# Fused linear attention and mixture-of-experts layer on one core: identity matmuls ahead of the tokens, a reordered start, and a shorter Newton step

## The reference, cut to what matters

```python
xn = _layernorm(x)                                   # (2, 512, 512) tokens
# attention: 32 heads of 128, causal, a decay per head
qkv = silu(xn @ qkv_w.T)
attn = linear_attention_with_decay(q, k, v)          # exp(-slope * distance) on the scores
attn = attn * rsqrt(mean(attn * attn, -1) + 1e-5)    # over all 4096 columns
a = (sigmoid(xn @ gate_w.T) * (norm_w * attn)) @ out_w.T
# experts: router, best 2 of 8, low-rank experts
logits = xn @ W_router.T
h = xn @ A ; hw = h * combine
f = xn @ W_base.T + b_base + 2 * hw @ B
return x + a + f
```

## Time and profile before

| | |
|---|---|
| median of 3 runs | 1084.96 us (1084.82 to 1085.02) |
| the profiled execution | 1084.91 us, its span 1083.0 us |
| busy share of the span: PE, PEld | 99%, 87% |
| DVE, ACT, POOL | 66%, 63%, 59% |
| chain that ended last, by engine | PE 95%, ACT 1%, DVE 1%, DMA 1%, POOL 1%, issue 1% |

### The profile page before, as it was taken

The page is one execution under the profiler, slowest core; times in us unless marked ns, Lnnn a source line. Parts: engine busy times, 40 slices in busy tenths (PEclk is TensorE's granted clock), DMA queues, the critical chain, the costliest instruction groups (busy, mean ns, idle before and its releaser), DMA issues.

```text
span 1083.0 us, 18994 instructions
## 1 busy us (share of the span) xinstructions
PE 1069.0 (99%) x5902; PEld 941.9 (87%) x5902; DVE 715.0 (66%) x1209; ACT 686.2 (63%) x1401; POOL 635.3 (59%) x625
## 2 busy tenths in 40 slices
PE   6999999999999999999999999999999999999998
PEld 5898889888898888988898888988889888898897
DVE  7777674666657676675756667475755757557567
ACT  8677565765667565675756766576656756567532
POOL 4747563584637657375544846367473764647744
DMA  8212020120201201021101102012020211112222
GB/s 300 66 35 93 25 64 20 45 64 25 64 19 54 71 25 62 3 84 39 56 32 44 63 24 63 19 44 63 24 71 12 82 44 44 44 38 71 60 82 78
DMA packets 41605, 60.04 MB, mean 55 GB/s; under 512 B 3936, under 2 KB 21600, under 8 KB 41568
## 3 DMA queue, kind: packets, MB, share of 16 engines
q1 hardware_dynamic: 40992, 59.01, 17.1%
q10 hardware_dynamic: 576, 0.56, 0.2%
HBM read 52.74 MB, written 6.82 MB: 55 GB/s over the span
## 4 chain that ended last, share of the span: by engine, by line
PE 95%; ACT 1%; DVE 1%; DMA 1%; POOL 1%; issue 1%; SPq 0%; DVEq 0%; POOLq 0%
PE bank_q L1809 8%; PE bank_q L1811 8%; PE bank_q L1810 8%; PE bank_p L1809 6%; PE bank_p L1811 6%; PE bank_p L1810 5%; PE bank_r L1809 5%; PE bank_r L1811 5%; PE bank_r L1810 5%; PE outp L1809 5%; PE outp L1810 5%; PE outp L1811 5%; PE score L1811 3%; PE score L1810 3%; PE score L1809 3%; PE att L1811 3%
## 5 line engine op out<-in xcount | busy, mean ns | idle before, releaser
L415 POOL TENSOR_TENSOR w_lo<-combo,w_hi 128x768 fp32r<-128x768 f32 (+1 forms) x128 | 166.7, 1311 | 155.4 <-ACT w_hi L611 155.3
L415 POOL TENSOR_TENSOR w_lo<-raw,w_hi 128x256 fp32r<-128x256 f32 (+1 forms) x128 | 131.9, 1032 | 123.9 <-ACT w_hi L611 123.4
L466 POOL TENSOR_TENSOR sum_sq<-sum_sq,square 128x512 f32<-128x512 f32 x64 | 82.7, 1293 | 65.4 <-ACT square L760 65.4
L1372 DVE TENSOR_TENSOR acc<-acc,outp 128x512 f32<-128x512 f32 x116 | 79.4, 684 | 62.1 <-PE outp L1811 61.3
L1810 PE MATMUL bank_q<-c_lo,w_hi 128*128 128x512 f32 x276 | 107.4, 389 | 0.0
L1811 PE MATMUL bank_q<-c_hi,w_lo 128*128 128x512 f32 x276 | 107.4, 389 | 0.0
L1809 PE MATMUL bank_q<-c_hi,w_hi 128*128 128x512 f32 x276 | 107.4, 389 | 0.0
L1282 DVE TENSOR_TENSOR score<-score,table 128x512 f32<-128x512 f32 (+1 forms) x128 | 75.9, 627 | 40.6 <-PE score L1811 39.6
L1230 DVE TENSOR_TENSOR xs<-bank_r,xs 128x512 f32<-128x512 f32 x64 | 44.2, 691 | 88.6 <-ACT xs L611 60.9
L611 ACT ACTIVATE p_hi<-score 128x896 fp32r<-128x896 f32 (+1 forms) x128 | 81.1, 649 | 33.7 <-DVE score L1282 33.0
L1809 PE MATMUL outp<-wo_hi,g_hi 128*128 128x512 f32 x250 | 97.7, 391 | 0.2 <-DVE acc L1372 0.2
(11 more groups left out here) (295 smaller groups left out, 3470.2 us busy)
## 6 DMA issues: line engine op xcount, KB each, us to landing
raw<-w_chunks SPq DMA_DIRECT2D x165, 256.0 KB, 2.8
near_dram<-near SPq DMA_DIRECT2D x2, 2048.0 KB, 8.9
table<-near_dram SPq DMA_DIRECT2D x32, 128.0 KB, 2.0
y<-x SPq DMA_DIRECT2D x8, 256.0 KB, 3.8
out<-acc SPq DMA_DIRECT2D x7, 256.0 KB, 2.0
acc<-x SPq DMA_DIRECT2D x6, 256.0 KB, 7.4
acc<-x ACTq DMA_DIRECT2D x2, 256.0 KB, 3.9
hw_dram<-acc SPq DMA_DIRECT2D x1, 512.0 KB, 2.9
```

Of the source, the lines that this page charges most:

```text
L415: pool.tensor_tensor(piece(w_lo[i % 2], j), piece_source(i, j), piece(w_hi[i % 2], j).bitcast(F32), ALU.subtract).then_inc(wlo[j], 1)
L466: pool.tensor_tensor(sum_sq[:, s % 2, :], sum_sq[:, s % 2, :], square[:], ALU.add).then_inc(summed, 1)
L1372: dve.tensor_tensor(tile, tile, outp, ALU.add).then_inc(acc_done, 1)
```

## The change

TensorE multiplies the identity by itself 16 times before it waits for the first tokens. Tiles 0 and 1 are loaded in halves by two queues. `slope` and `norm` move from ScalarE's queue to the end of SyncE's first loads. `refine` has 3 operations in place of 4. q and k of batch 0 are made by passes over both (high parts of everything first). ScalarE makes one decay table fewer ahead of the first weights, and copies all 8 token tiles before `first_q(0)`; V1's weights come after. GpSimd's `combine(V1)` waits until all tiles are normalised, and the token sum `t_raw[:, 2]` goes ahead of V1's low parts. VectorE does `first_lows(0)` after the first token sum. `first_gates(1, 1)` goes ahead of V2's weights. In the last body `make_c22(G01)` goes ahead of `inverse_root(1, 1)`.

```diff
 @block.sync
-            for t in (0, 2):
-                sp.dma_start(acc[:, t, :], x_tok[:, t, :]).then_inc(x_in[t], 16)
+            for t in range(2):
+                sp.dma_start(acc[0:P // 2, t, :], x_tok[0:P // 2, t, :]).then_inc(x_in[t], 16)
+            sp.dma_start(acc[:, 2, :], x_tok[:, 2, :]).then_inc(x_in[2], 16)
             load_rows(0, 0, 3)
...
             sp.dma_start(ar[:], a_router).then_inc(ar_in, 16)
+            sp.dma_start(slope[:], slopes.rearrange("(a h) -> a h", a=1).to_broadcast([P, HEADS])).then_inc(slope_in, 16)
+            sp.dma_start(norm[:], norm_w).then_inc(norm_in, 16)
 @block.gpsimd
+            pool.wait_ge(xn_ready, NTB)
             combine(V1)
+            pool.wait_ge(xt_done, NTB)
+            pool.tensor_tensor(t_raw[:, 2], x_t[:, 2:4, 1, :], x_t[:, 0:2, 1, :], ALU.subtract).then_inc(t3_made, 1)
             low(V1, 2)
             low(V1, 4)
-            pool.wait_ge(xt_done, NTB)
-            pool.tensor_tensor(t_raw[:, 2], x_t[:, 2:4, 1, :], x_t[:, 0:2, 1, :], ALU.subtract).then_inc(t3_made, 1)
 @block.scalar
-            for t in (1, 3):
-                act.dma_start(acc[:, t, :], x_tok[:, t, :]).then_inc(x_in[t], 16)
-            act.dma_start(slope[:], slopes.rearrange("(a h) -> a h", a=1).to_broadcast([P, HEADS])).then_inc(slope_in, 16)
-            act.dma_start(norm[:], norm_w).then_inc(norm_in, 16)
+            for t in range(2):
+                act.dma_start(acc[P // 2:P, t, :], x_tok[P // 2:P, t, :]).then_inc(x_in[t], 16)
+            act.dma_start(acc[:, 3, :], x_tok[:, 3, :]).then_inc(x_in[3], 16)
-            nears(range(16))
+            nears(range(15))
             act.wait_ge(raw_in[0], 32)
...
             tokens_hi(0)
+            nears((15,))
+            tokens_hi(1)
             nears((16,))
-            tokens_hi(1)
-            nears((17,))
             tokens_hi(2)
             tokens_hi(3)
...
-            nears(range(18, HEADS))
+            nears(range(17, HEADS))
...
-            for t in range(3):
+            for t in range(TB):
                 tokens_whole(t)
-            tokens_whole(3)
-            first_q(0)
-            first_k(0)
-            weight(V1, 2)
             tokens_hi(4)
             tokens_hi(5)
             tokens_whole(4)
-            weight(V1, 4)
...
             tokens_whole(7)
+            first_q(0)
+            first_k(0)
+            weight(V1, 2)
+            weight(V1, 4)
...
             first_gates(1, 0)
+            first_gates(1, 1)
             weight(V2, 2)
             weight(V2, 1)
             weight(V2, 3)
-            first_gates(1, 1)
 @block.vector
                 link(dve.tensor_tensor(a, y_, y_, ALU.mult))
-                link(dve.tensor_tensor(b, a, v, ALU.mult))
-                link(dve.tensor_scalar(a, b, -0.5, 1.5, ALU.mult, ALU.add))
-                root = dve.tensor_tensor(y_, y_, a, ALU.mult)
+                link(dve.scalar_tensor_tensor(out=b, in0=a, scalar=-0.5, in1=v, op0=ALU.mult, op1=ALU.mult))
+                root = dve.scalar_tensor_tensor(out=y_, in0=b, scalar=1.5, in1=y_, op0=ALU.add, op1=ALU.mult)
...
+                    make_c22(G01)
                     inverse_root(1, 1)
-                    make_c22(G01)
...
-            first_lows(0)
...
             dve.tensor_tensor(t_raw[:, 0], x_t[:, 0:2, 1, :], x_t[:, 0:2, 0, :], ALU.subtract).then_inc(t1_made, 1)
+            first_lows(0)
 @block.tensor
-            first_rows(0, 0)
-            first_rows(1, 0)
+            first_head()
+            pe.wait_ge(consts, 2)
+            for _ in range(16):
+                pe.matmul(outp[:, 0:P], ident[:], ident[:], start=True, stop=True, skip_group_check=True)
             pe.wait_ge(consts, CONSTS)
             for t in range(TB):
                 turn_tokens(t)
```

More of the change, by code:

```diff
@@ L1721, in measure @@
             def measure(t):
-                dve.wait_ge(x_in[t], 16)
+                dve.wait_ge(x_in[t], 32 if t < 2 else 16)
                 dve.bn_stats(stats[:, t, :], acc[:, t, :]).then_inc(ln, 1)
@@ L2107, in first_rows @@
             def first_rows(r, b):
-                if (r, b) == (0, 0):
-                    first_q_rows()
-                    return
                 pe.wait_ge(first_wlo, r // 2 + 1)
@@ L2126, in first_rows, with first_head, q, k @@
                 mm.then_inc(first_ready, 1)
-            def first_q_rows():
-                for half in range(2):
+            def first_head():
+                def q(half, w_, b_, first, last):
                     tok = slice(256 * half, 256 * half + 256)
-                    pe.wait_ge(xh_done, 2 * half + 2)
                     for kc in range(KC):
                         w = slice(kc % 2 * P, kc % 2 * P + P)
-                        pe.matmul(bp[:, tok], first_hi[:, 0, kc // 2, w], b_hi[:, kc // 2, kc % 2, tok], start=half == 0 and kc == 0,
-                                  stop=False, skip_group_check=True)
-                    pe.wait_ge(first_qlo, 1)
+                        mm = pe.matmul(bp[:, tok], w_[:, 0, kc // 2, w], b_[:, kc // 2, kc % 2, tok], start=first and half == 0 and kc == 0,
+                                       stop=last and kc == KC - 1, skip_group_check=True)
+                    return mm
+                def k(w_, b_, first, last):
@@ L2138, in first_q_rows @@
                     for kc in range(KC):
                         w = slice(kc % 2 * P, kc % 2 * P + P)
-                        pe.matmul(bp[:, tok], first_lo[:, 0, kc // 2, w], b_hi[:, kc // 2, kc % 2, tok], start=False,
-                                  stop=False, skip_group_check=True)
+                        mm = pe.matmul(bq, w_[:, 0, 2 + kc // 2, w], b_[:, kc // 2, kc % 2, :], start=first and kc == 0,
+                                       stop=last and kc == KC - 1, skip_group_check=True)
@@ L2142, in first_q_rows @@
+                    return mm
+                pe.wait_ge(first_whi, 2)
+                for half in range(2):
+                    pe.wait_ge(xh_done, 2 * half + 2)
+                    q(half, first_hi, b_hi, True, False)
+                k(first_hi, b_hi, True, False)
+                pe.wait_ge(first_qlo, 1)
+                for half in range(2):
+                    q(half, first_lo, b_hi, False, False)
+                for half in range(2):
                     pe.wait_ge(xl_done, 2 * half + 2)
-                    for kc in range(KC):
-                        w = slice(kc % 2 * P, kc % 2 * P + P)
-                        mm = pe.matmul(bp[:, tok], first_hi[:, 0, kc // 2, w], b_lo[:, kc // 2, kc % 2, tok], start=False,
-                                       stop=kc == KC - 1, skip_group_check=True)
+                    mm = q(half, first_hi, b_lo, False, half == 1)
@@ L2147, in first_q_rows @@
                 mm.then_inc(first_ready, 1)
+                k(first_hi, b_lo, False, False)
+                pe.wait_ge(first_wlo, 1)
+                k(first_lo, b_hi, False, True).then_inc(first_ready, 1)
+            pe.wait_ge(consts, 2)
+            for _ in range(16):
+                pe.matmul(outp[:, 0:P], ident[:], ident[:], start=True, stop=True, skip_group_check=True)
             pe.wait_ge(consts, CONSTS)
```

## The result

The changed kernel took 1087.88 us (median of 20 runs, 1085.55 to 1089.51), the kernel before beside it 1085.18 (20 runs, 1084.26 to 1087.03). The ratio is 1.0022, with a 95% interval of 1.0016 to 1.0029: **slower by 2.7 us** (0.22%, clear of the interval), where 3.4 us of gain were forecast (1081.5, range 1080.8 to 1083.0). The profiled execution took 1088.58 us, 3.7 more than the one of before.

A forecast was written before the change was run, and what follows sets the result against it. TensorE, busy 1069.0 of 1083.0 us, bounds the kernel, with its start bound by ScalarE. 1084.91 - 2.55 (start) - 0.8 (end) = 1081.56, stated as 1081.5; range 1080.8 to 1083.0.

The forecast's parts named there:

- Edits at nothing: Reordered q, k, V1's and V2's weights, token sums, `slope` and `norm`: priced at 0, with up to 0.5 us against.
- my fourth rival: New TensorE waits behind 28.85 us, for V1's or V2's weights or token sums: gain handed back, 1084.2 to 1085; chance 0.06.
- First tokens: First token loads: half tiles gain 0.3 us; with Newton's step, normalising begins 0.5 earlier, first transpose at 8.7, not 9.22.
- my first rival: At the start, TensorE's clock stays low or falls back before the transposes: 1082.3 us; chance 0.14.
- ScalarE's list as bound of the start: ScalarE's work sets when `first_rows(0, 1)` begins: 28.85 in place of 31.39, 2.55 us gained.
- The closed DMA gap: First weight loads: without small packets of `slope` and `norm` ahead, worth 1.1 us, `raw[0]` landing by 8.2.
- The identity matmuls: Ahead of the first tokens: end at 8.2, clock then high, a tile's four transposes take 0.65 us, not 1.07.
- The end: Product 3 of the last unit: its 0.9 us wait for `make_c22` goes, 0.8 gained, lower end 0.4.
- Newton's step: Ahead of normalising the first tokens: one of four linked operations fewer, 0.2 us with the gap to the next.
- the new order of the start: ScalarE's last whole token copy ends at 26.7, 3.9 us earlier; q of batch 0 comes last, ending at 28.85.

The follow-up runs named there:

- a2: The changed kernel with token tiles 0 and 1 loaded whole again: 1084.66 us, ratio to the kernel before 0.9998.
- a3: The changed kernel with whole tiles 0 and 1 and `first_gates(1, 1)` behind V2's weights again: 1082.55 us, ratio to the kernel before 0.9981.
- b3: The kernel before with only `first_gates(1, 1)` moved ahead of V2's weights: 1088.48 us, ratio 1.0032.
- b2: The kernel before with only tiles 0 and 1 loaded in halves of 64 partitions by two queues: 1086.39 us, ratio 1.0014.
- a1: The changed kernel with `first_gates(1, 1)` behind V2's weights again, half tiles kept: 1084.03 us, ratio to the kernel before 0.9997.
- d1: The changed kernel without its 16 identity matmuls: 1088.68 us, ratio to the kernel before 1.0027.
- d0: The changed kernel, unchanged, measured again beside its variants on one chip: 1087.76 us, ratio to the kernel before 1.0024.
- c3: The changed kernel with the gate behind V2's weights and both 64-partition halves of a tile on one queue: 1084.25 us, ratio to the kernel before 0.9995.
- a4: The changed kernel with whole tiles, the gate behind V2's weights and no identity matmuls: 1083.13 us, ratio to the kernel before 0.9985.
- b1: The kernel before with only `make_c22(G01)` moved ahead of `inverse_root(1, 1)`: 1084.57 us, ratio 0.9993.
- b5: The kernel before with only `slope` and `norm` moved to the end of SyncE's first loads: 1084.71 us, ratio 0.9998.
- c1: a3 with piece 1 of V2's weights made first on GpSimd and ScalarE: 1082.52 us, ratio to the kernel before 0.9974.
- c2: The changed kernel with the gate behind V2's weights and tiles halved by columns, on two queues: 1083.35 us, ratio to the kernel before 0.9982.

## Why the prediction was wrong, point by point

**The step that failed is "Edits at nothing".** It priced V2's weights behind `first_gates(1, 1)` at 0, with up to 0.5 against, on the ground that TensorE had waited for none of them and "no row shows how near they were". The trace of before did show it, in a row that I had not picked: the low parts stood in its timeline, done some 0.3 us ahead of their use at 47.79. I read their use as V2's, later in `body(0)`; it is the first product of V1. The moved gate costs 2.1 us out of the changed kernel (a2 less a3; 1.9 among runs at 1.000) and 3.2 into the old one (b3). The mechanism was in my fourth rival, at 0.06, whose price ended at "the gain is handed back"; it can go beyond, since the wait has no tie to what the start gained.

**"First tokens" failed too.** Halves were to bring 0.3, at worst 0; they cost 1.3 (b2) to 1.5 (a1 less a3). My bounds were made from the landings of whole tiles, as if a form that no row shows could only reorder bytes. The sentence of the Trainium skill that I weighed ("DMA: Bandwidth & Descriptors", Issuing engines are not separate DMA queues: two issuers save only issue time) left room for no gain; the loss came from the form, at which the DMA engines moved 201 GB/s where they had moved 393, and not even the issue time was saved: two halves take 1.48 us to issue where two tiles took 0.90.

**The clock, my first rival, came in another shape.** It fell not because the transposes don't count, but after TensorE's own waits: 3.3 us ahead of the transposes in the profile of after, 2.2 us ahead of V1's product in d1. The kernels sort by the largest wait behind TensorE's first work, as the one profiled execution of each shows it (3.3 in after and 2.2 in d0, which are one kernel). With one of 1.9 to 3.3 us the clock was lower in 16 of 20 (after), 7 of 11 (d0), 5 of 6 (d1), 5 of 11 (a2), 5 of 11 (c3), 2 of 6 (b3), 2 of 11 (a1); with none above 1.1 us in none (a3, a4, b1, b2, b5, c1, c2, before). In the changed kernel the runs with and without a fall are 2.5 us apart (medians 1088.46 and 1085.95); part of that is the late tiles, as said at d0. Why one such wait brings the fall in one run and not in the next stays open. A wait alone is enough (d1, without the identity matmuls), and the identity matmuls alone are not (a3, with no long wait behind them: none of 11); that the fall at 12.4 takes both is suggested by b2 against a1 and c3, and not shown.

**Adding up.** a3_both is 2.26 under before. Put back the gate (+2.11) and the halves (+1.48): +1.33. Measured is +2.70. With runs at 1.000 alone the same sum is 1.86 + 1.36 - 2.26 = +0.96, and the runs of the changed kernel at 1.000 are +0.77 (after) and +0.86 (d0): so without the falls the sum closes. The rest of the 2.7 is in the runs with a fall: 23 of 31 with both waits, and with one of them 2 of 11 (a1), 5 of 11 (a2), 5 of 11 (c3), 2 of 6 (b3) and 5 of 6 (d1).

**What held.** ScalarE's list as bound of the start: without the two parts every landmark is as forecast or a little earlier, the first transpose at 8.89 (8.7), `tokens_whole(0)` at 19.30 (19.4), `q_lo` and then `first_rows(0, 1)` at 28.51 (28.85), 2.63 gained for 2.55 (from 31.14, its real start before, and not from 31.39). The closed DMA gap: weights ready by 7.6 (8.2), shown alone by b5. The identity matmuls end at 7.67 in the profile of after and at 7.96 to 8.86 in the other seven that have them (8.2), in a3 only just ahead of the first transpose, and the transposes run at the high level, 8 in 1.06 us; the case in which the clock never rises ahead of them did not come. The end: the wait is gone, 0.86 in b1's profile, 0.5 in its median. Newton's step was not tried alone; from its first operation to `normalise` it takes 0.59 us in the trace of after and 0.79 in that of before, the 0.2 of the forecast. Nor was the new order of the start (`first_head`, the whole copies, the token sums) tried without the rest.

**What a3_both still lacks** of the forecast (1082.55 for 1081.5): 0.46 is the wait for `w_lo` behind GpSimd's full list, which c1 takes away (0.3 us by the medians); TensorE also waits 0.3 for `acc` in the loop. The remainder is not explained.

## What to carry to other kernels

Before an operation is moved ahead of another on an engine, look up the first reader of what then comes later, by its wait in the code and not by its name, and measure the slack between its completion and that reader: here 0.3 us, under a move of 2.5. A transfer of a form that the trace doesn't hold can cost as well as give, so its lower bound is not zero; try it alone first. And a wait of 2 us of TensorE can cost more than its length: 3.2 us for a wait of 2.2 in b3, and the clock may fall behind it.

## What the runs showed of the hardware

- A transfer of a token tile's half over 64 partitions took 0.74 us to issue on ScalarE's queue and 0.61 on SyncE's, the whole tile over 128 partitions or its half by columns 0.45. While such halves ran, from 3 to 4 us, the 16 DMA engines moved 201 GB/s (after; 182 in c3), with whole tiles 393 (before), with halves by columns 368 (c2). The bytes came late too: VectorE waited for its third and fourth tile until 7.89 in the changed kernel; with whole tiles (a3) it measured them at 5.80, straight behind the others.
- Two transfers of 16 KB, each to 128 partitions in small packets, issued ahead on another queue, held back two weight chunks: the second landed 7.2 us after its issue with it (before) and 5.0 without (b5), and from 5.7 to 7.2 us the DMA engines moved 101 and 358 GB/s.
- After a wait of 2.19 us in otherwise full work the granted clock went from 1.00 to 0.50 (1.2 GHz) about 1.2 us after TensorE had resumed, for about 3 us (d1). The Trainium skill ("TensorE: Matmul & The Clock Gate", Part 1: The HAM clock gate) says that the gate follows how busy TensorE has been lately; the run agrees, and adds that a wait of 2.19 us was enough in some executions and not in others (5 of 6 in d1, 2 of 6 in b3).
